# Moving buffers in SBUF, so that each stationary operand starts 128 bytes from its moving one, counted by 256

## The reference, cut to what matters

```
h = layernorm(x) * (1 + ca) + sa
Q, K = elu(h Wq' + bq) + 1, elu(h Wk' + bk) + 1 ;  V = h Wv' + bv     # 16 heads of 16
out  = Q (K'V) / (Q sum(K) + 1e-6)                                    # linear attention, per head
x    = x + ga * (out Wo' + bo)
h = layernorm(x) * (1 + cb) + sb
gates = softmax over the two best of 8 of (cosine(h, centroids) + h w_route')
x    = x + gb * sum_e gates[e] * (gelu(h w1[e] + b1[e]) w2[e] + b2[e])   # all 8 experts, 256 -> 128 -> 256
```

## Time and profile before

| | us |
|---|---|
| median of 3 runs | 363.16 |
| span of the profiled execution, first to last instruction | 360.9 |
| median less span (what lies around the instructions) | 2.3 |
| TensorE matmuls busy | 346.5 |
| weight loads busy | 324.3 |
| VectorE / GpSimd / ScalarE busy | 286.6 / 259.4 / 234.7 |

### The profile page before, as it was taken

One profiled execution on the slowest core, in us unless ns is written; L12 is line 12 of the kernel. 1 busy time (PEld: TensorE's weight loads), 2 busy tenths in 40 slices (PEclk: granted clock), 3 DMA queues, 4 the chain that ended last, 5 costly groups with the idle time before them and its releaser, 6 DMA issues.

```text
span 360.9 us, 8816 instructions
## 1 busy us (share of the span) xinstructions
PE 346.5 (96%) x2790; PEld 324.3 (90%) x2790; DVE 286.6 (79%) x819; ACT 234.7 (65%) x517; POOL 259.4 (72%) x358
## 2 busy tenths in 40 slices
PE   8899999998999988799999999999999999999995
PEld 8667888887888977799998999999999999999895
DVE  5589676658748889989999889898898888876754
ACT  4685878887877745756747476584574765855541
POOL 4367999977867587787897878988889867755210
PEclk9999999999999999999999999999999999999999
DMA  8953630000000033133242322421323214214311
GB/s 266 331 167 94 192 96 0 2 3 0 2 0 3 4 117 119 56 93 105 55 136 80 69 91 61 147 85 63 130 65 97 88 60 145 91 61 145 98 51 61
DMA packets 23715, 31.82 MB, mean 88 GB/s; under 512 B 2288, under 2 KB 14204, under 8 KB 23680
## 3 DMA queue, kind: packets, MB, share of 16 engines
q1 hardware_dynamic: 23240, 31.34, 28.2%
q10 hardware_dynamic: 440, 0.04, 0.1%
HBM read 27.04 MB, written 4.34 MB: 87 GB/s over the span
## 4 chain that ended last, share of the span: by engine, by line
PE 73%; DVE 17%; issue 4%; ACT 3%; DMA 1%; POOL 1%; DVEq 0%; ACTq 0%; POOLq 0%
PE bank L797 20%; PE bank L798 19%; PE bank L799 19%; PE bank L805 4%; PE bank L852 3%; DVE hid_g L1355 2%; PE bank L829 2%; PE bank L981 2%; DVE bank L1372 2%; DVE early L1272 1%; DVE gT_f L1411 1%; DVE den L1303 1%; PE bank L1023 1%; PE bank L908 1%; DVE qz_lo L1310 1%
## 5 line engine op out<-in xcount | busy, mean ns | idle before, releaser
L740 ACT ACTIVATE bank<-bank,cols_sb 128x256 f32<-128x256 f32 x128 | 51.3, 438 | 43.3 <-PE bank L799 43.0
L797 PE MATMUL bank<-tr_hi,w_hi 128*128 128x256 f32 x256 | 73.4, 287 | 0.0
L798 PE MATMUL bank<-tr_lo,w_hi 128*128 128x256 f32 x256 | 72.3, 282 | 0.0
L799 PE MATMUL bank<-tr_hi,w_lo 128*128 128x256 f32 x256 | 72.1, 282 | 0.0
L797 PE MATMUL bank<-w_hi,hid_pair 128*128 128x256 f32 x252 | 70.5, 280 | 0.0
L799 PE MATMUL bank<-w_hi,hid_pair 128*128 128x256 f32 x252 | 70.3, 279 | 0.0
L798 PE MATMUL bank<-w_lo,hid_pair 128*128 128x256 f32 x252 | 70.2, 279 | 0.0
L501 POOL TENSOR_TENSOR hid_pair<-hid_g,hid_pair 128x512 fp32r<-128x512 f32 x42 | 54.3, 1292 | 7.0 <-POOL gT_r L526 3.3
L797 PEld LDWEIGHTS bank<-tr_hi,w_hi 128*128 128x128 f32 x256 | 48.8, 191 | 0.3 <-DVE hid_g L1355 0.2
L799 PEld LDWEIGHTS bank<-tr_hi,w_lo 128*128 128x128 f32 x256 | 48.9, 191 | 0.0
L798 PEld LDWEIGHTS bank<-tr_lo,w_hi 128*128 128x128 f32 x256 | 48.8, 191 | 0.0
(11 more groups left out here) (162 smaller groups left out, 928.3 us busy)
## 6 DMA issues: line engine op xcount, KB each, us to landing
g_bc<-g_dram SPq DMA_DIRECT2D x64, 256.0 KB, 3.5
x_sb<-in_x SPq DMA_DIRECT2D x16, 256.0 KB, 3.0
out<-x_sb SPq DMA_DIRECT2D x15, 256.0 KB, 2.3
early<-in_wmod SPq DMA_DIRECT2D x3, 512.0 KB, 7.0
q_sb<-in_w SPq DMA_DIRECT2D x2, 512.0 KB, 6.5
q_sb<-in_w SPq DMA_DIRECT2D x1, 1024.0 KB, 9.5
mod_row<-mod_dram SPq DMA_DIRECT2D x1, 1024.0 KB, 6.2
q_sb<-in_wqkvT SPq DMA_DIRECT2D x2, 384.0 KB, 5.3
```

The costliest lines, as they stand in the source:

```text
L740: last = ac.activation(half, half, ACT.Gelu, bias=b1_sb[:, e:e + 1])
L797: te.matmul(out_ap, l_hi, r_hi, start=start, stop=False, skip_group_check=shared)
L798: te.matmul(out_ap, l_hi, r_lo, start=False, stop=False, skip_group_check=shared)
L799: return te.matmul(out_ap, l_lo, r_hi, start=False, stop=stop, skip_group_check=shared)
```

## The change: what it does

No instruction is added, taken away or put elsewhere on any engine: all 3713 instructions of the program text (loops counted once) stand in the same order, with the same operations, sizes and semaphore waits. Only addresses (and two tensors' names) differ. Unused tensors are allocated between the buffers (`skip`), 1024 bytes a partition in all, and w_hi and w_lo become w1_hi, w1_lo, w2_hi and w2_lo, each of 8 slots, so that w1 and w2 can have different places.

```diff
+        def skip(name, n_bytes):
+
+            sb(name, [P, n_bytes // 4])
...
         m_lo = sb("m_lo", [P, B, NC, E], F32R)
+        skip("ahead_of_qz", 128)
         qz_hi = sb("qz_hi", [P, NC, E], F32R)
...
+        skip("ahead_of_bqk", 256)
         bqk_r = sb("bqk_r", [P, 2 * E], F32R)
...
-        w_hi = sb("w_hi", [P, 2 * NE, E], F32R)
-        w_lo = sb("w_lo", [P, 2 * NE, E], F32R)
-        w1_hi, w1_lo = (m[:, 0:NE, :].rearrange("p (c g) (k j) -> p c (g k) j", c=NC, k=E // HID)
-                        for m in (w_hi, w_lo))
-        w2_hi, w2_lo = (m[:, NE:2 * NE, :] for m in (w_hi, w_lo))
+        skip("ahead_of_w1", 192)
+        w1_parts = [sb(name, [P, NE, E], F32R) for name in ("w1_hi", "w1_lo")]
+        w1_hi, w1_lo = (m[:, :, :].rearrange("p (c g) (k j) -> p c (g k) j", c=NC, k=E // HID) for m in w1_parts)
+        skip("ahead_of_w2", 128)
+        w2_parts = [sb(name, [P, NE, E], F32R) for name in ("w2_hi", "w2_lo")]
+        w2_hi, w2_lo = w2_parts
         b2_r = sb("b2_r", [P, E], F32R)
+        skip("ahead_of_route", 128)
         route_r = sb("route_r", [P, NC, 4 * NE], F32R)
...
+        skip("ahead_of_tr", 128)
         tr_hi = sb("tr_hi", [P, 3, NC, 2 * P], F32R)
         tr_lo = sb("tr_lo", [P, 3, NC, 2 * P], F32R)
...
+        skip("ahead_of_gates", 64)
         gT_f = sb("gT_f", [4 * NE, 2, 2 * P])
         gT_r = sb("gT_r", [P, 2, 2 * P], F32R)
...
+        def weight_rows(i, part):
+
+            if isinstance(i, int) and i >= NE:
+                return w2_parts[part][:, i - NE:i - NE + 1, :]
+            return w1_parts[part][:, bass.ds(i, 1), :]
...
-                hi = w_hi[:, bass.ds(i, 1), :]
+                hi = weight_rows(i, 0)
...
-                TT(w_lo[:, bass.ds(i, 1), :], src, hi.bitcast(F32), ALU.subtract).then_inc(w_ready, 1)
+                TT(weight_rows(i, 1), src, hi.bitcast(F32), ALU.subtract).then_inc(w_ready, 1)
```

More of the change, by code:

```diff
@@ L618, in cast_weights @@
                 act.wait_ge(d_w, 48)
-                ac.activation(w_hi[:, i, :], w_raw[:, i, :], ACT.Copy).then_inc(w_hi_end, 1)
+                ac.activation(weight_rows(i, 0), w_raw[:, i:i + 1, :], ACT.Copy).then_inc(w_hi_end, 1)
             def negative_part(u, t):
```

## The result

The changed kernel takes 364.28 us (median of 6 runs, 364.04 to 364.43), the kernel before, on the same chip, 363.12 (6 runs, 362.56 to 363.51). The ratio is 1.0034, with an interval of 1.0023 to 1.0044: slower, though by little. The forecast was 357.4 us. In every run here the time is 1.7 to 1.9 us more than the span, so the trace of before, with a span of 360.9 us, is of a run somewhat faster than the median, and that of after, with 362.7, of the slowest of the six. (The 2.3 us that the forecast added to the span is therefore some 0.5 too large; 5.8 us off the median give the same 357.4.)

A forecast was written before the change was run, and what follows sets the result against it. TensorE's row of matmuls, by its pace, was taken as the bound nearly everywhere; 10.0 us of terms by 0.8 by 0.73 gave 5.8 us less: span 355.1, with 2.3 us around it 357.4 us, range 354.8 to 364.0.

The forecast's parts named there:

- the value taken between the bounds: For places now 128 apart on TensorE: four fifths of the 10.0 us lower-bound saving, one fifth kept back.
- the sum: TensorE time saved at undisturbed pace: first 4.6, second 2.5, attend 1.2, v 0.6, qk and bias 1.1; 10.0 us.
- The bounds: Pace of matmuls 128 apart: lower 113.4 ns, undisturbed, 7.3 us saved at the end; upper 126.6 ns, 12.5 us slower.
- 73%: TensorE's share of the chain that ended last, taken as the part of its saved time that reaches the end.
- the point from which the sum turns: Mean present pace of 960 matmuls at 119 and 948 at 116.3: 117.7 ns; above that the kernel is slower.
- The third rival: Every mm3: at 128 apart a load meets the matmul in mid-stream; 12.5 us slower, 375.7 us; chance 0.14.
- The first rival: 128 only as good as 64 apart: first and attend fall to 279.3 ns, 1.9 us saved, 361.3 us; chance 0.24.
- the second rival: Place doesn't decide TensorE's pace, what ran before may; nothing changes, 363.2 us; chance 0.19.
- The carried pace: First stage's slow pace carries into second: 117.5 ns behind a first stage, 113.5 behind transposes; less without 0-apart places in the loop.
- The cover: In stage e, a unit falls to 13.84 us; GpSimd's 12.48 and VectorE's 12.39 stay hidden, 1.4 us over.

The follow-up runs named there:

- the map: Kernel before with matmul series added behind its work, stationary operand 0 to 4096 bytes from moving at 25 distances; 120.0 ns at 0, 118.5 at 128; span grows some 180 us.
- second_back_to_64: The changed kernel with w2 alone put back 64 bytes from hid; 363.13 us, ratio 0.9998 to the kernel before.
- only_first_to_64: The kernel before with w1 alone moved, to stand 64 bytes behind tr; 361.03 us, ratio 0.9945 to the kernel before.
- all_64: Layout with stationary operands of mm3, bias, gates and route 64 bytes behind their moving ones; 361.54 us, ratio 0.9955 to the kernel before.
- all_0: Layout with both operands of every matmul of mm3, bias, gates and route at the same place by 256; 365.18 us, ratio 1.0065 to the kernel before.
- the second map: The same matmul series behind the kernel before's work, at distances 4 to 12, 36 to 92 and 196 to 236 bytes in steps of 4; 117.7 ns at 64.

## Why the prediction was wrong

**The step that failed first is the value taken between the bounds**: "I take a value near the lower bound: four fifths of the sum", with "128 is as far apart as two places can be by 256" as its reason. It was to take 4.8 ns off each matmul of first and attend and 2.6 off second. Measured from starts, first lost 0.7 ns (6.0 to 5.3 above 113.3), attend 0.8, and second became slower by 2.7 (2.65 to 5.39). The terms of the sum come out as -0.5, -0.15 and +2.1 us, with v at +0.3, qk unchanged, and 0.2 more from route and the gates: +1.9 instead of -8. Two rows, 0 and 64, were read as a slope and drawn on to 128; the map shows that there is no slope.

**The bounds** held: 118.6 lies between 113.4 and 126.6. A value between the three paces that the trace showed for full loads (113.5, 117.5 and 120, in the mean 117) would have given little change, since the point from which the sum turns is 117.7. At 118.6 the sum by that step is 0.9 ns times 1908 matmuls, 1.7 us more of TensorE's time, where 1.9 came, and at 73% 1.3 us at the end, where the medians differ by 1.2. The places 128 apart lie close together, first at 118.6, second at 118.7 and attend at 118.4; v stands off with 119.5.

**The third rival** had the right sign and the right turning point, with a chance of 0.14, and 12.5 us for a price that is 1.2 at the end. (The 13 ns of its upper bound come from starts rounded to 10 ns; the matmul at 48.47 took 236 ns to the next start, 9 more than 226.8.) Its mark, means over 283 ns, was not met, and its mechanism, a load that meets the matmul in the middle of its stream, is not shown: the map has 118.5 at 128, but 120.0 at 144 and 116.7 at 208. **The first rival** fails because 128 is not as good as 64; second_back_to_64 shows that second's place alone makes the loss. **The second** fails on the map. By the Trainium skill, "TensorE: Matmul & The Clock Gate", Part 2, loading the next weights takes no read bandwidth from the running matmul. Here paces from 113.3 to 121 ns were measured with the same tiles, clock and neighbours, by the distance alone. So what the second rival drew from that rule, that no address can matter, does not hold for these operands; what a load and a matmul contend for, no run shows.

**The carried pace** was right as far as it went: 64 runs at 117.7 behind a row at 0, and at 113.3 behind transposes in the first map, though not in the second, and only_first_to_64 gives second the better pace without touching its place by 256. But moving to 128 ended the fast pace of second, which was the better half of what it had.

**The cover** was the second wrong step, masked in this result by the first. "VectorE with 12.39 still fit, with 1.4 us over": it did not, as all_64 shows. TensorE's time fell by 5.4 us there, 3.9 by the 73%, and the time by 1.6. Had the forecast paces come, its saving of 8 us would by the same share have brought 2.4 us, an estimate, and a time near 361, not 357.4. The mistake lay in "without a stop of TensorE": a wait shorter than the overlap of two matmuls (0.16 us) leaves no idle time in a window, and VectorE's busy time leaves out what passes between its instructions. Of a loss some three fifths reached the end (1.2 us of 1.9 here, 2.4 of 3.7 in all_0), of a gain less than a third to under a half (1.6 of 5.4 in all_64, 2.0 of 4.4 in only_first_to_64). That fits two engines that hold a unit together, of which a slower TensorE sets the time and a faster one waits for VectorE; by how much in which unit was not worked out.

**Left open**: by what mechanism the distance sets the pace, why 64 has two paces and what else than a row at 0 brings the slower. The map says what each distance costs here, not why. In all_64 nothing stands 0 apart, and yet 21 of second's 62 rows ran at 117.6 to 118. Stage a's qk and v stand 64 bytes ahead of wqkv in before, which the map counts as 192 (117.7 ns there), and 64 behind in all_64. By this v got the fast pace in part: 118 ns in 15 of 16 units before, 114 to 115 in nine and 118 in seven in all_64. The qk matmuls did not gain (231.2 ns for 512 columns in before, 233.1 in all_64), and no run tells why.

## What to carry to other kernels

A place in SBUF is worth measuring, not extrapolating: run the matmul at a dozen distances in one kernel and take the best, moving only the buffer that gains (here w1; 0.55% for 64 bytes). When an operand already shows two paces in a trace, moving it can lose the better one. And before counting on an engine's slack, look for late starts at its hand-overs, and for matmuls that last longer than their neighbours: a busy share of 100% on the one engine and 86% on the other did not mean that the second had time.

## What the runs showed of the hardware that was not expected

- The pace of 256-column matmuls in float32r with a 128-column load beside each depends on where the stationary operand starts against the moving one, counted by 256 bytes: 120.0 ns at 0, 118.5 at 128, 116.7 at 208 and 224, 113.3 or 117.7 at 64. Steps of 4 bytes change it by up to 6 ns, in no order that can be read from the map.
- 64 bytes apart has two paces, 113.3 and 117.7 ns, and a row of twelve matmuls at 0 leaves it at the slower; it took the slower one elsewhere too, in the second map behind transposes.
- At 128 apart the starts repeat a pattern of five (115, 117, 122, 120, 119 ns; mean 118.6), in first, second and attend alike; v, 128 apart too, has 119.5 in the mean.
- The loads' duration does not tell the pace: 188 ns goes with 113.4 in before and with 118.6 in after.
